# Eight norms run batch by batch inside the stage that makes their rows; weights of the next feed-forward stage are loaded during the stage ahead

## The reference

```
for layer in 0..3:
    x = x + tanh(g_xattn[layer]) * attention(layer, layernorm(x), ctx)
    x = x + tanh(g_ffn[layer])   * feed_forward(layer, layernorm(x))
```

## Time and profile before

| | us |
|---|---|
| median of 3 runs | 3257.74 (3253.65 to 3259.48) |
| the profiled execution | 3253.4 |
| its span | 3251.7 |
| PE busy | 2631.7 |
| DVE busy | 1991.1 |
| ACT busy | 1318.7 |
| POOL busy | 952.4 |

### The profile page before, as it was taken

How to read it: one execution, slowest core, us unless ns; L and a number is a source line. 1 busy time by engine, 2 the same in 40 slices (tenths; PEclk the granted TensorE clock), 3 DMA queues, 4 the chain that set the end, 5 groups by cost and what they waited for, 6 DMA issues and landing times. The chain is left out here.

```text
span 3251.7 us, 59049 instructions
## 1 busy us (share of the span) xinstructions
PE 2631.7 (81%) x21112; PEld 2038.8 (63%) x21112; DVE 1991.1 (61%) x3992; ACT 1318.7 (41%) x2568; POOL 952.4 (29%) x845
## 2 busy tenths in 40 slices
PE   7997797969969998694996927866766994899995
PEld 7996476946856665362774624543444773788884
DVE  5555785148852223485874058788777765677775
ACT  4443565235641111464564103333334552455552
POOL 3443200020002222454001024355342002666672
PEclk9998798988979999797897968988977995999998
DMA  7887563346510000524650020000025642454553
GB/s 221 244 246 236 162 185 98 134 144 162 151 64 1 1 0 16 146 69 124 161 150 32 0 78 1 1 0 0 0 76 151 167 104 95 176 185 189 200 200 99
DMA packets 152553, 363.33 MB, mean 112 GB/s; under 512 B 25969, under 2 KB 109809, under 8 KB 136609
## 3 DMA queue, kind: packets, MB, share of 16 engines
q1 hardware_dynamic: 140592, 275.12, 29.8%
q0 software_dynamic: 11760, 85.51, 7.4%
HBM read 271.42 MB, written 88.67 MB: 111 GB/s over the span
## 5 line engine op out<-in xcount | busy, mean ns | idle before, releaser
L934 ACT ACTIVATE arena<-ps 125x448 f32<-125x448 f32 x768 | 409.6, 545 | 354.3 <-PE ps L853 347.5
L959 DVE TENSOR_REDUCE arena<-ps 112x2 f32<-112x750 f32 x384 | 349.7, 934 | 82.7 <-PE ps L837 76.9
L476 POOL TENSOR_SCALAR ln_tmp<-ln_tmp 112x16 f32<-112x16 f32 x11 | 2.9, 262 | 984.2 <-DVE ln_tmp L444 984.2
L837 PE MATMUL ps<-wreg,arena 96*112 96x375 bf16 x768 | 217.8, 372 | 90.4 <-DMA arena<-query_parts 50.8
L2383 PE MATMUL ps<-moe_x_r,moe_w_r 128*128 128x256 f32 x2016 | 255.3, 287 | 18.3 <-DVE arena L2535 16.8
L2383 PEld LDWEIGHTS ps<-moe_x_r,moe_w_r 128*128 128x128 f32 x2016 | 246.9, 192 | 23.7 <-DVE arena L2535 20.3
L853 PEld LDWEIGHTS ps<-arena,wreg 98*125 98x125 bf16 x2304 | 213.0, 142 | 62.6 <-issue 25.8
L853 PE MATMUL ps<-arena,wreg 98*125 98x112 bf16 x2304 | 235.5, 227 | 3.0 <-ACT arena L934 3.0
L1964 POOL TENSOR_TENSOR arena<-arena 112x1024 f32<-112x1024 f32 x64 | 156.5, 2453 | 227.9 <-DVE arena L2078 161.4
L498 PE MATMUL ps<-ident,xn 112*128 112x112 f32 x320 | 73.2, 385 | 183.3 <-DVE xn L457 138.2
L863 PE MATMUL ps<-arena 125*17 125x112 f32 x6144 | 200.2, 264 | 0.6 <-ACT arena L934 0.6
(11 more groups left out here) (320 smaller groups left out, 5879.9 us busy)
## 6 DMA issues: line engine op xcount, KB each, us to landing
wreg<-key_parts SPq DMA_DIRECT2D x288, 187.5 KB, 3.9
key_parts<-arena SPq DMA_DIRECT2D x128, 281.2 KB, 4.0
arena<-query_parts SPq DMA_DIRECT2D x108, 224.0 KB, 4.6
values<-arena SPq DMA_DIRECT2D x64, 357.0 KB
arena<-values SPq DMA_DIRECT2D x64, 357.0 KB
arena<-key_parts SPq DMA_DIRECT2D x96, 187.5 KB, 3.6
query_parts<-arena SPq DMA_DIRECT2D x48, 336.0 KB, 2.5
wreg<-in_e_w SPq DMA_DIRECT2D x16, 704.0 KB, 5.3
```

What stands on the lines that cost most here:

```text
L837: mm = pe.matmul(ps[0:T, 2 * (p % 2) + e, 0:S2], queries(b)[0:SROWS, hd, :], keys[r][0:SROWS, hd, :], start=True, stop=True)
L934: act.activation(probs[k % PROBS], ps[0:KN, 4 + k % 2, 0:GT], ACT.Exp, scale=scale).then_inc(at_probs, 1)
L959: dve.tensor_reduce(negmax[r % 2][:, 2 * p:2 * p + 2], ps[0:T, 2 * (p % 2):2 * (p % 2) + 2, 0:S2], AX.X, ALU.max, negate=True).then_inc(at ...
```

## The change

`norm_stage` is called twice only: at the start and behind the position experts. The nine others become nine `RowNorm` objects, one in each of the four cross-attention stages, the self-attention, the low-rank experts and the product-key stage, and two (`inner`, `outer`) in the ReLU stage. Each stage calls its steps for a batch where it has just added that batch: `stats` and `moments` on DVE, `deviation` on POOL for one batch (three operations, two with a gain), then without a gain `apply` on ACT, with a gain `scale` on DVE; `turn` on PE and `evacuate` on ACT. Every loop in these stages is written out. In a step b of a cross-attention stage the norm of b-1 is begun, that of b-2 applied and that of b-3 turned; what is left of the last batches stands behind the loop.

The weight loads of four feed-forward stages move: SP issues those of the position experts (the first expert, 4 transfers), the low-rank experts (7 of 10) and the ReLU stage in step 12 of the cross-attention stage ahead (`load_ahead`), and those of the product-key stage during the ReLU stage, into memory which the earlier stage leaves free and on semaphores of their own.

```diff
@@ norm_stage becomes RowNorm @@
+        class RowNorm:
+            def load(self, sp):
+                if self.gain is not None:
+                    for r in range(2):
+                        sp.dma_start(ln_gain[:, r, :], a["ln_rows"][self.gain + r].partition_broadcast(128)).then_inc(loaded, 16)
...
+            def stats(self, dve, b, sem, value):
+                dve.wait_ge(sem, value)
+                dve.bn_stats(ln_raw[:, b, :], self.src[:, b, :]).then_inc(ln_stat, 1)
+
+            def moments(self, dve, b):
+                dve.wait_ge(ln_stat, self.before("stat", b) + 1)
+                dve.bn_aggr(ln_mv[:, b, :], ln_raw[:, b, :]).then_inc(ln_step, 1)
+
+            def deviation(self, pool, b):
+                r = self.before("ready", b)
+                rstd = ln_rstd[:, b:b + 1]
+                pool.wait_ge(ln_step, self.before("step", b) + 1)
+                pool.tensor_scalar(ln_var[:, b:b + 1], ln_mv[:, b, 1:2], self.eps, None, ALU.add).then_inc(ln_ready, 1)
+                pool.wait_ge(ln_ready, r + 1)
+                pool.tensor_tensor(rstd, ln_var[:, b:b + 1], half[:, b:b + 1], ALU.pow).then_inc(ln_ready, 1)
+                if self.gain is None:
+                    pool.wait_ge(ln_ready, r + 2)
+                    pool.tensor_scalar(ln_shift[:, b:b + 1], ln_mv[:, b, 0:1], rstd, -1.0, ALU.mult, ALU.mult).then_inc(ln_ready, 1)
+
+            def apply(self, act, b):
+                act.wait_ge(ln_ready, self.before("ready", b) + 3)
+                if self.keep is None:
+                    at_least(act, ln_turned, self.before("turned", b) - XN + 1)
+                act.activation(self.rows(b), self.src[:, b, :], ACT.Identity, bias=ln_shift[:, b:b + 1],
+                               scale=ln_rstd[:, b:b + 1]).then_inc(ln_normed, 1)
+
+            def scale(self, dve, b):
...
+                dve.scalar_tensor_tensor(ln_scale[:, b % XN, :], self.src[:, b, :], ln_mv[:, b, 0:1], ln_gain[0:T, 0, :],
+                                         ALU.subtract, ALU.mult).then_inc(ln_scaled, 1)
+                dve.wait_ge(ln_scaled, self.before("scaled", b) + 1)
+                dve.scalar_tensor_tensor(self.rows(b), ln_scale[:, b % XN, :], ln_rstd[:, b:b + 1], ln_gain[0:T, 1, :],
+                                         ALU.mult, ALU.add).then_inc(ln_kept, 1)
...
+            def turn(self, pe, b, view, slots):
...
+                for c in range(DC):
+                    mm = pe.transpose(view[:, c * T:(c + 1) * T], self.rows(b)[:, c * 128:(c + 1) * 128], ident[0:T, 0:T])
+                mm.then_inc(ln_turned, 1)
+
+            def evacuate(self, act, b, view):
+                act.wait_ge(ln_turned, self.before("turned", b) + 1)
+                act.activation(xn_t[:, :, b * T:(b + 1) * T], view.rearrange("p (c t) -> p c t", c=DC), ACT.Copy).then_inc(ln_evac, 1)
@@ cross_stage, SP @@
+                    if load_ahead is not None and b == B - 4:
+                        load_ahead(sp)
@@ cross_stage, PE @@
-                        if k == 1 and has(b, 1):
+                        if k == 0:
                             at_least(pe, o_added, last if has(b, -1) else o0)
+                            if has(b, -3):
+                                norm.turn(pe, b - 3, turned, 1)
+                        if k == 2 and has(b, 1):
+                            if has(b, -3):
+                                norm.evacuated(pe, b - 3)
                             maxima(b + 1, place(1))
@@ cross_stage, ACT @@
+                        if k == 6 and has(b, -2) and norm.gain is None:
+                            norm.apply(act, b - 2)
+                        if k == 1 and has(b, -3):
+                            norm.evacuate(act, b - 3, turned)
@@ cross_stage, DVE @@
+                        if p == 1 and has(b, -2):
+                            norm.moments(dve, b - 2)
+                        if p == 5 and has(b, -2) and norm.gain is not None:
+                            norm.scale(dve, b - 2)
+                        if p == 7 and has(b, -1):
+                            norm.stats(dve, b - 1, o_added, last + 1)
@@ chain @@
-            norm_stage(h, 1e-6, gain=2, keep=h)
-            relu_stage()
-            norm_stage(h, 1e-6, gain=4, turn=False, add_gate=2)
-            norm_stage(x, 1e-5)
-            product_key_stage(6)
+            following = ProductKeyWeights()
+            relu_stage(dict(eps=1e-6, gain=4, turn=False, add_gate=2), dict(eps=1e-5), weights, following)
+            product_key_stage(6, dict(eps=1e-5), following)
```

More of the change, by code:

```diff
@@ L63, in clear, with place @@
         self.at = 0
+    def place(self, at, parts, *dims):
+        self.at, kept = at, self.at
+        view = self.take(parts, *dims)
+        self.at = kept
+        return view
     def take(self, parts, *dims, dtype=F32):
@@ L773, in sync @@
             def sync(sp):
+                norm.load(sp)
                 def load_masks(b, r):
@@ L942, in scalar @@
                 out.copy_turned(act, o0 + B - 1, (B - 1) % 2)
+                for b in range(B - 3, B):
+                    if norm.gain is None and b > B - 3:
+                        norm.apply(act, b)
+                    norm.evacuate(act, b, ps[:, b % 2, 0:DC * T])
             def vector(dve):
                 dve.memset(ps[:, SUMS, :], 0.0)
+                if norm.gain is not None:
+                    dve.wait_ge(loaded, rows_ready)
                 out.add_bias(dve)
@@ L1161, in tensor @@
                 out.project(pe, o0 + B - 1, 1)
+                for b in range(B - 4, B):
+                    norm.turn(pe, b, turned, 1)
             def scalar(act):
@@ L1864, in step, with turn @@
                             queries(g + 1)
+                def turn(g, first):
+                    for q in range(first, first + 2):
+                        norm.turn(pe, g * GB + q, slots[q % 2], 2)
                 def embeddings(g, q):
@@ L1952, in scalar @@
                 over_groups(act, step)
+                for q in range(GB):
+                    norm.apply(act, (G - 1) * GB + q)
+                    norm.evacuate(act, (G - 1) * GB + q, slots[q % 2])
             def gpsimd(pool):
-                pool.memset(keys, 0.0).then_inc(const_made, 1)
                 def step(g):
```

528 lines of the change are left out of this document (350 added, 178 removed).

## The result

The changed kernel takes 3180.41 us (median of 4 runs, 3176.35 to 3183.59) against 3257.01; the ratio is 0.9768, with a 95% interval of 0.9753 to 0.9784. 3212 was forecast, in a range of 3172 to 3252, so the direction and the range hold and the gain, 76.6 us, was underrated by 31. Measured a second time, the same kernel took 3190.01 against 3258.12, ratio 0.9787 (0.9757 to 0.9818), a gain of 68.1.

A forecast was written before the change was run, and what follows sets the result against it. Norm chains bound the fronts; PE bounds cross-attention and masked loops, DVE self-attention. 185.6 - 70.3 (loops) - 46.5 (tails) - 23 (clock) = 45.8 us off 3253.4: 3207.6, plus 4.3 for the median: 3212, range 3172 to 3252.

The forecast's parts named there:

- The fronts: Nine stretches between a stage's last work and the next's first matmul, 216.9 us in sum; 185.6 us were to go.
- The maxima's wait and the turn: Cross-attention loop: PE's wait at `maxima` for ACT's copy, 0.60, and the turn, 0.19; 0.79 us a batch, 10.3 a stage.
- The rival that it is not seen: Cross-attention and masked loops: PE pays only the turns, 29 us more gain, 3183 (band 3170 to 3195); chance 0.17.
- tails of cross-attention: The last batch's norm chain between last addition and barrier: 4.0 us in each of four cross-attention stages.
- Self: Self-attention loop: DVE gains 1.58 us a batch and idles 0.69, so 0.9 a batch, 11.5 in sum; bounds 0 and 20.5.
- the clock: Stage starts: real work at PE's lower clock, twice the time per matmul, costing 23 us; bounds 10 and 50.
- ReLU: ReLU stage: fronts of 32.6 and 37.0 give 32.0 and 37.0; 3.0 for turns, 15.8 tail, 2.4 clock come back.
- Product-key: Product-key stage: front gain 18.9; DVE's and ACT's additions cost 9 (bounds 0 and 20), tail 6, clock 2.
- Routed: Front of 20.5 us ahead of the routed stage: 3.0 left for its own router load, gain 17.5.
- DVE held up by POOL: All of POOL's 1.2 us a batch lies on DVE through the shared port lock: +25 us, 3237; chance 0.12.
- The clock falls in the loops: PE's new waits lower its clock in cross-attention steps, 7.4 us each; 3330 with 16 falls; chance 0.09.
- Loads that collide: Row maxima of batch 14 queue behind weight loads on SP; three stages lose up to 10 us each: 3242; chance 0.07.

The follow-up runs named there:

- cross_copy_0: Changed kernel with ACT's copy of the norm behind exponential 0 of a cross-attention step in place of exponential 1: 3166.25 us, ratio 0.9705 to the kernel before.
- self_norm_apart: Changed kernel with the self-attention's norm alone as a block between that stage and the next queries: 3183.66 us, ratio 0.9782 to the kernel before.
- self_copy_2: Changed kernel with ACT's copy of batch b-5 in quarter 2 of a self-attention step in place of quarter 3: 3185.50 us, ratio 0.9776 to the kernel before.
- three_places_warm: Changed kernel with cross-attention and self-attention copies a slot earlier, ReLU's steps interleaved, and five unread matmuls in three query stages: 3150.97 us, ratio 0.9678.
- loads_late: Changed kernel with weights of position, low-rank, ReLU and product-key loaded at the head of their own stages: 3236.88 us, ratio 0.9939 to the kernel before.
- before_again: The kernel before, unchanged, run once more for its profile: one run of 3248.63 us.
- norms_apart: Changed kernel's loads ahead, but the nine norms as blocks between the stages, with the same steps per batch: 3321.73 us, ratio 1.0206 to the kernel before.
- loads_only: As norms_apart, but POOL makes the deviations of all 16 batches in four operations: 3285.29 us, ratio 1.0091 to the kernel before.

## Why the prediction was right, and by how much it missed

**The fronts** were priced at 185.6 and gave about 188: what is left is 0.2 or less where I took 0.6, and 5.6, 7.3, 7.2, 5.8 and 3.0 where I took 5.9, 7.2, 7.3, 6.1 and 3.0.

**The maxima's wait and the turn**: 0.79 a batch forecast, 0.76 measured (11.31 - 10.55), and cross_copy_0 splits it into 0.2 and 0.56. The rival that it is not seen falls. In the masked stage 1.0 was forecast and 0.89 measured (14.66 - 13.77). The tails of cross-attention were 4.0 forecast, 3.8 measured.

**What was luck.** The middle of the forecast was 3195 to 3232, and 3180 lies outside of it, in the band of 3170 to 3195 that I had given to the rival whose mechanism did not come. The mechanisms were right, but several terms were priced too high; that the result still lies in the range is owed to the range's width.

**Self**: 0.9 a batch forecast, 0.75 measured against the kernel before and 0.94 against the written-out loop without the norm (self_norm_apart). That the copy did not cost it was shown by self_copy_2. The bound was named too simply, as DVE alone.

**The term that was mis-sized most is the clock**, 23 us in sum. The four stages in which it can be read apart, with front and tail taken off, became longer by 1.8 (position, 118.3 to 120.1) and 1.1, 1.5 and 1.2 (the query stages), 5.6 together, where I had 15.7. The other terms, 7.4 for low-rank, ReLU and product-key, can't be read apart. I had priced half-speed matmuls at their full loss; in the query stages the matmuls at full speed shortened the stage by less than the loss, as three_places_warm shows. 10 of the 27 us by which the spans' difference exceeds 45.8 are this.

**ReLU** cost 16.5 behind its front, not 21.2, with a tail of 14.3 in place of 15.8. **Product-key** cost 11.3 (10 in the second pair of profiles), not 17: the sum of DVE's and ACT's additions was partly hidden, as the bound of 0 had left open; which part, I did not test. **Routed** gave 22.3, not 17.5; like paired with like it gave 14.9 or 19.8, so its term was about right. These are 15 of the 27; the fronts' 2, and cross-attention (4.9), against self (3) and small ones, the rest. Cross-attention's 4.9 is no error of the prediction either: 6.2 us are the stretched batch of the first profile before (206.9 for 200.7). So some 10 of the 27 are chance of the two executions, and the second pair of spans (3246.9 and 3186.8) is only 14 us beyond the forecast.

**The rivals.** *DVE held up by POOL* did not come. In self-attention and in cross-attention 2, where the rival was priced, no POOL instruction ran during any of the 64 steps with gain, so they test nothing. In ReLU 12 of the 32 such steps ran beside POOL, and there it is POOL that becomes longer:

```profile
1774.57 0.47 DVE L491 SCALAR_TENSOR_TENSOR ln_scale<-h,ln_mv,ln_gain 112x256 f32<-112x256 f32 x1
1774.75 0.37 POOL L469 TENSOR_SCALAR ln_var<-ln_mv 112x1 f32<-112x1 f32 x1 [2.58 <-DVE ln_mv L463]
...
1775.08 0.48 DVE L494 SCALAR_TENSOR_TENSOR ln_scale<-ln_scale,ln_rstd,ln_gain 112x256 f32<-112x256 f32 x1
...
1775.19 0.78 POOL L471 TENSOR_TENSOR ln_rstd<-ln_var,half 112x1 f32<-112x1 f32 x1
...
1775.48 0.48 DVE L491 SCALAR_TENSOR_TENSOR ln_scale<-h,ln_mv,ln_gain 112x256 f32<-112x256 f32 x1
```

DVE keeps its 0.47 to 0.49. POOL's addition takes 0.37 to 0.40, in ReLU's other batches 0.22, and its power 0.78, there 0.57; both end within 0.1 us behind a step of DVE. The Trainium skill, SBUF — State Buffer, section "SBUF: two separate sides", says of the two engines' shared ports that one of them blocks while the other has them. The trace agrees, but POOL is the one that waits, where the prediction had charged DVE.

*The clock falls in the loops* came in a small part. The granted clock is 1.00 in the steady batches, and a wait of 0.4 per batch in the unmasked stages did not bring it down. But in both profiles of the changed kernel one masked batch took 17.6 in place of 14.66, at a clock of 0.82, and no masked batch of the kernel before did; low-rank had 3.4 us at the lower level behind its start in one profile and 13.7 in the other, the kernel before none there behind its first 38 us. That is 3 us in the masked stage and up to 4 in low-rank (351.3 and 355.4); and self-attention's 164.3 and 159.2 go with 48 and 33 us of it at the lower level. *Loads that collide*: not seen; the last three full batches of cross-attention 0 take 11.31 each with the loads behind them and without (loads_late).

The prediction did not say that the two halves of the change need each other, though its own condition held it: it took from each front "what is left when the norm is done and the feed-forward weights are there".

## What to carry to other kernels

A front in which a computation and a transfer run side by side costs the longer of the two: taking one away wins only what it was longer. Here the loads alone won nothing that can be told (0.9994, interval to 1.0013), the norms alone 0.6% after what they cost the loops, and both 2.3%. When serial work is folded into a loop, look up which instruction of the bounding engine waits for the new one, and put the new one a slot earlier: moving one copy by one exponential gave 16 us by stages and 24 by medians, a fifth to a third of the whole change. Then check with the waits whether the stall vanished or only moved, as in self-attention. And profile each kernel twice before dividing a difference among its parts: here a third of what the forecast missed in the first pair of profiles was chance.

## What the runs showed of the hardware

One DVE group of the routed stage, untouched by the change, takes two different times in different executions of one program: the kernel before and, below it, the same in before_again.

```profile
L2535 DVE SCALAR_TENSOR_TENSOR arena<-arena 128x256 f32<-128x256 f32 x168 | 162.7, 978 | 59.6 <-ACT arena L2430 48.2
```

```profile
L2535 DVE SCALAR_TENSOR_TENSOR arena<-arena 128x256 f32<-128x256 f32 x168 | 140.5, 846 | 62.1 <-ACT arena L2430 60.9
```

The changed kernel showed 848 ns, then 985 ns. All fourteen profiles have one of the two times, whatever the kernel, and runs on one chip share it: 985 to 987 in the four on one chip, 846 to 849 in the four on a second, 845 to 848 in the three on a third, 986 in the one on a fourth (for the first two profiles the chip is not known). Where the routed stage is the changed one it takes 528.2 to 529.1 us in the five executions with the short time and 533.5 to 536.5 in the four with the long one. So the time went with the chip and not with the program; what differs there stays open.

POOL's power costs 0.57 us on one column and 2.94 on sixteen: 0.16 a column above a fixed 0.4. A norm done by batch pays 9 us for it in place of 3, which was seen only where POOL stands on the chain (norms_apart).

POOL's short operations become longer beside some of DVE's and not beside others. Beside the steps with gain (L491, L494) it is 0.57 to 0.78 for the power and 0.22 to 0.40 for the addition; in low-rank the addition takes 0.50 beside a DVE copy of 896 columns (L1821), and the last of the three operations 0.86 in place of 0.26 beside two products (L1825). Beside reductions (L1050, L1344) and beside steps that read PSUM (L1370) addition and power kept 0.22 and 0.57.

ACT's application with a scale and an offset per row (L481) takes 0.59 us on 112x256, where the copy of the same shape took 0.41 to 0.44 in the kernel before; I had taken 0.4. In the loops it is hidden; in a block of its own it is a part of why loads_only was slow.
